# Q5 of the last two groups as seven 256x256x256 products, with its sums put together apart and added to the output in double tiles

## The reference

```python
W = L0_cond_weights[itok_B_0_15]                  # (64, 64, 64), one of 16 per batch element
y = einsum('bct,bcd->bdt', x, W)                  # conditioning, per batch element 64x64
xf = y.reshape(-1, 1024)                          # 4096 rows
scores = xf @ Wr.T                                # 64 experts of rank 16
top_vals, top_idx = top_k(scores, 16)
G = zeros((4096, 64)).at[rows, top_idx].set(softmax(top_vals))
h = einsum('nd,krd->nkr', xf, A)                  # 4096 x 1024 by 1024 x 1024
out = einsum('nkr,kdr->nd', h * G[:, :, None], B) # 4096 x 1024 by 1024 x 1024
return x + 2.0 * out
```

## Time and profile before

| | us |
|---|---|
| three runs | 708.48, 707.5, 706.84 (median 707.5) |
| the profiled execution | 707.46, of it span 705.7 |
| PE busy in the span | 700.4 (99%) |
| PEld busy | 608.5 (86%) |
| DVE busy | 568.8 (81%) |
| ACT busy | 292.2 (41%) |
| DMA | 301 GB/s on average |

### The profile page before, as it was taken

One profiled execution on the slowest core, in us unless ns is written; L12 is line 12 of the kernel. 1 busy time (PEld: TensorE's weight loads), 2 busy tenths in 40 slices (PEclk: granted clock), 3 DMA queues, 4 the chain that ended last, 5 costly groups with the idle time before them and its releaser, 6 DMA issues.

```text
span 705.7 us, 11098 instructions
## 1 busy us (share of the span) xinstructions
PE 700.4 (99%) x3822; PEld 608.5 (86%) x3822; DVE 568.8 (81%) x1022; ACT 292.2 (41%) x541; POOL 15.8 (2%) x22
## 2 busy tenths in 40 slices
PE   8999999999999999999999999999999999999998
PEld 8888888888888888988999888898899988888897
DVE  5888998897757899889795867987668496699885
ACT  5575554534535541444333542242334364233220
POOL 0000000100000000010000000001000000000100
PEclk9999999999999999999999999999999999999999
DMA  8976679787899998979989775868769987666886
GB/s 314 405 291 279 211 281 401 229 261 268 332 382 417 415 359 290 406 255 325 388 312 412 285 271 189 301 247 245 248 274 372 380 311 258 199 217 211 228 329 239
DMA packets 68937, 212.35 MB, mean 301 GB/s; under 512 B 10706, under 2 KB 13394, under 8 KB 68242
## 3 DMA queue, kind: packets, MB, share of 16 engines
q1 hardware_dynamic: 64802, 204.30, 78.0%
q0 software_dynamic: 2304, 4.20, 3.9%
q10 hardware_dynamic: 1776, 3.15, 1.2%
HBM read 150.80 MB, written 65.01 MB: 306 GB/s over the span
## 4 chain that ended last, share of the span: by engine, by line
PE 99%; DMA 1%; DVE 0%; issue 0%; DVEq 0%
PE Pb L755 40%; PE Pb L788 29%; PE Pb L809 13%; PE Cb L737 8%; PE S L852 4%; PE Pb L831 3%; DMA xc<-in_wts 1%; PE S L844 1%; PE T L907 0%; PE T L913 0%; PE Pb L771 0%; PE Cb L866 0%; PE S L866 0%; PE T L866 0%; DVE Q L1212 0%
## 5 line engine op out<-in xcount | busy, mean ns | idle before, releaser
L755 PE MATMUL Pb<-Op,Wt 128*128 128x512 f32 x888 | 214.2, 391 | 0.0
L755 PEld LDWEIGHTS Pb<-Op,Wt 128*128 128x128 f32 x888 | 165.4, 188 | 33.9
L788 PE MATMUL Pb<-Wt,Op 128*128 128x512 f32 x744 | 179.7, 391 | 0.0
L788 PEld LDWEIGHTS Pb<-Wt,Op 128*128 128x128 f32 x744 | 138.1, 188 | 28.1 <-DVE Op L1212 0.4
L1212 DVE TENSOR_TENSOR Q<-Pb,Q 128x512 f32<-128x512 f32 (+1 forms) x105 | 92.8, 901 | 27.9 <-issue 17.5
L1212 DVE TENSOR_TENSOR Op<-R,Op 128x512 fp32r<-128x512 f32 x100 | 66.6, 686 | 23.4 <-ACT Op L945 23.3
L755 PE MATMUL Pb<-Ox,Wt 128*128 128x512 f32 x300 | 75.3, 390 | 0.0
L998 ACT COPY R<-Cb 128x512 f32<-128x512 f32 x60 | 35.1, 587 | 91.2 <-PE Cb L737 91.2
L755 PEld LDWEIGHTS Pb<-Ox,Wt 128*128 128x128 f32 x300 | 56.0, 188 | 11.5
L945 ACT CAST Op<-R 128x512 fp32r<-128x512 f32 x100 | 58.3, 622 | 17.3 <-DVE R L1212 10.4
L1212 DVE TENSOR_TENSOR Cq<-Pb,Cq 128x1024 f32<-128x1024 f32 (+1 forms) x46 | 44.5, 966 | 24.3 <-issue 10.4
(11 more groups left out here) (118 smaller groups left out, 688.9 us busy)
## 6 DMA issues: line engine op xcount, KB each, us to landing
Wt<-Wd SPq DMA_DIRECT2D x201, 512.0 KB, 6.5
Wd<-Wt SPq DMA_DIRECT2D x56, 512.0 KB, 5.1
xc<-in_x SPq DMA_DIRECT2D x24, 512.0 KB, 5.4
Q<-in_x SPq DMA_DIRECT2D x16, 512.0 KB, 5.3
out<-Q SPq DMA_DIRECT2D x8, 1024.0 KB, 4.8
BR<-in_B SPq DMA_DIRECT2D x4, 1024.0 KB, 8.5
Q<-in_x SPq DMA_DIRECT2D x16, 256.0 KB, 5.6
out<-in_x SPq DMA_DIRECT2D x16, 256.0 KB, 5.9
```

The lines of the kernel that those rows point to most:

```text
L755: t = e.matmul(Pb[:, j, :], Wt[:, k, a, 128 * c:128 * c + 128], part((USES1[m], s, c), z), start=fresh and (c, a, z) == (0, 0, 0), stop=(c ...
L788: t = e.matmul(Pb[:, i, :], part((USES2[m], s, c), a)[:, 128 * i:128 * i + 128], Wt[:, k, z, :], start=fresh and (c, a, z) == (0, 0, 0), s ...
```

## The change

In groups 2 and 3 `TWO` becomes (0, 4, 5, 6): Q5, too, is computed in seven forms. For this:

- seven more made units (level 5) are made in the first half of group 2, in steps 12 to 15 (P3) and 20 to 22 (P7). Their source T1b, a weight sum that group 0 computes, is stored to a DRAM tensor in group 0 and read back into BR in group 2;
- S1 is split in seven pieces; its four sums (`sum_five`) are made in Q4's stage (in group 3 two of them in Q7's), on semaphore v_ysum;
- Q5's forms use the banks of `BANK1` (3, 0, 3, 2, 3, 2, 3). They aren't added to Q but put together in Cq[:, 0], S1's place: ScalarE copies forms 0, 2, 3 and 6, VectorE adds forms 1, 4 and 5 (`drain_five`);
- the whole is then added to Q by four adds of a double tile (128x1024, `add_five`), two into Q5's place and two into Q3's, which stand in Q3's stage at steps 0, 1, 2 and 4. At steps 0 and 1 they stand ahead of the splits, and Q3's drain stands behind these;
- the splits of S1, S4 and the next group's y21 are spread anew over Q4, Q5 and Q3 on VectorE (`lows_second`), and `sum_y` moves within Q5's stage;
- the two 1 MB stores of rows 0 to 3 move from Q5's stage to steps 0 and 3 of Q3's, behind `add_five`;
- the first form of the next group's P2 waits for ScalarE's copy of Q5's form 6.

```diff
-TWO = [(), (0, 4, 6), (0, 4, 6), (0, 4, 6)]
+TWO = [(), (0, 4, 6), (0, 4, 5, 6), (0, 4, 5, 6)]
-LEVEL = (4, 6, 0, 7)
+LEVEL = (4, 6, 0, 7, 5)
+           7: [8, 9, 10, 12, 13, 14, 20], 5: [12, 13, 14, 15, 20, 21, 22]}
 def splits_second(s, m, c):
-        return [("G22", c + 5)] if c < 2 else [("S1", c - 2)] if c < 6 else []
+        return [("G22", c + 5)] if c < 2 else [("S1", c - 2)] if c < 6 or 5 in TWO[s] else []
+    if m == 5 and m in TWO[s]:
+        return [("S1", c + 5) if c < 2 else ("S4", c - 2)]
+def lows_second(s, m, c):
+    if 5 not in TWO[s] or m < 4:
+        return splits_second(s, m, c)
+    if m == 4:
+        return [("G22", c + 5)] if c < 2 else [("S1", c - 4)] if c > 3 else []
+    if m == 5:
+        return [("S1", c + 3)] * (c < 4) + [("S4", k) for k in ((), (), (0,), (), (1,), (2,), (3, 4))[c]]
+    return [("S4", c + 5)] if c < 2 else [("y21", k) for k in ((), (0,), (), (1,), (2, 3, 4))[c - 2] if s + 1 < NS]
...
+                        if (s, step) == (2, 6):
+                            e.wait_ge(v_made, 28)
+                            e.wait_ge(l_b[1], 32)
+                            e.wait_ge(l_b[2], 32)
+                            e.dma_start(raws[2], T1b).then_inc(l_b[4], 16)
+                        if s == 0 and step in (17, 19):
+                            n = (step - 17) // 2
+                            e.wait_ge(v_bsum["T1b"], 2 * n + 2)
+                            e.dma_start(T1b[:, 2 * n:2 * n + 2, :], BR[:, 0, 2 * n:2 * n + 2, :]).then_inc(l_b[1 + n], 16)
+                        if 5 in TWO[s] and m == 6 and i in (0, 3):
+                            n = 1 if i == 0 else 0
+                            e.wait_ge(v_out, out_done(s, 5, n, 1))
+                            q_store(s, 2 * n, 0, 1024)
+                        if m == 5 and m in TWO[s]:
+                            continue
...
+                if m > 4 and 5 in TWO[s] and k in (0, 1, 3):
+                    if m == 5:
+                        e.wait_ge(v_out, out_done(s, *{0: (3, 3, 1), 1: (4, 1), 3: (4, 5)}[k]))
+                    else:
+                        e.wait_ge(v_out, out_done(s, *{0: (4, 6), 1: (5, 1), 3: (5, 5)}[k]))
...
+                        elif m == 5 and m in TWO[s] and i in (0, 2, 3, 6):
+                            e.wait_ge(p_two, form_done(s, 5, i))
+                            e.wait_ge(v_lo["S1"], split_done("S1", s, {0: 0, 2: 1, 3: 5, 6: 5}[i]))
+                            e.wait_ge(v_ysum, s1sum_done(s, "t4"))
+                            e.copy(five(i), Pb[:, BANK1[i], :].rearrange("p (i n) -> p i n", n=256)).then_inc(a_out, 1)
...
+            def drain_five(s, r):
+                if r in (1, 4, 5):
+                    e.wait_ge(p_two, form_done(s, 5, r))
+                    e.wait_ge(*in_output(s, 5, {1: 0, 4: 3, 5: 2}[r]))
+                    add(five(r), Pb[:, BANK1[r], :].rearrange("p (i n) -> p i n", n=256), five(r), v_out)
+            def add_five(s, n, name):
+                e.wait_ge(v_out, out_done(s, 5, 5))
+                e.wait_ge(*in_output(s, 5, 6))
+                tile, half = INTO[name][0] + 2 * n, INTO[name][1]
+                to = Q[:, tile:tile + 2, 512 * half:512 * half + 512]
...
+                add(to, Cq[:, 0, 2 * n:2 * n + 2, :], to, v_out)
...
+                            if m > 4 and 5 in TWO[s]:
+                                if m == 6 and c == 0:
+                                    add_five(s, 1, "Q5")
+                                elif m == 6 and c == 1:
+                                    add_five(s, 0, "Q3")
+                                if m == 6 and c > 1:
+                                    drain_two(s, m, c)
+                                for name, k in lows_second(s, m, c):
+                                    lo(name, s + (name == "y21"), k)
+                                if m == 6 and c < 2:
+                                    drain_two(s, m, c)
+                                elif m == 6 and c == 2:
+                                    add_five(s, 0, "Q5")
+                                elif m == 6 and c == 4:
+                                    add_five(s, 1, "Q3")
+                                if m == 5:
+                                    if c < 2:
+                                        sums_two(s, 6, SUMS2[c + 2])
+                                    drain_five(s, c)
+                                    if 1 < c < 6 and s + 1 in ONE:
+                                        sum_y(s + 1, SUMS2[c - 2])
```

More of the change, by code:

```diff
@@ L99, in ones, with fives @@
     return sum(r in ONE for r in range(s))
+def fives(s):
+    return sum(5 in TWO[r] for r in range(s))
 def cond_step(s, m, i):
@@ L232, in level_before, with sums_before, ysum_done, s1sum_done @@
     return sum(len(TWO[r]) for r in range(s)) + TWO[s].index(m)
+def sums_before(s, m):
+    return 4 * (level_before(s, m) - fives(s + (m > 5)))
 def y21_done(s, c):
     return 4 * s + 4 * ones(s) + c + 1
+def ysum_done(s, name):
+    return 4 * (ones(s) + fives(s)) + SUMS2.index(name) + 1
+def s1sum_done(s, name):
+    return 4 * (ones(s + 1) + fives(s)) + SUMS2.index(name) + 1
+def banks_two(m):
+    return BANK1 if m == 5 else BANK2
 def split_done(name, s, c):
@@ L257, in outs @@
                 copied += [(s, m, i, 0) for i in range(4)]
+            elif m == 5 and m in TWO[s]:
+                copied += [(s, m, i, 0) for i in (0, 2, 3, 6)]
+                order += [(s, m, i, 0) for i in (1, 4, 5)]
+            elif m == 6 and 5 in TWO[s]:
+                order += [(s, 5, 1, 1), (s, 6, 0, 0), (s, 5, 0, 2), (s, 6, 1, 0), (s, 6, 2, 0), (s, 5, 0, 1), (s, 6, 3, 0),
+                          (s, 6, 4, 0), (s, 5, 1, 2), (s, 6, 5, 0), (s, 6, 6, 0)]
             elif m in TWO[s]:
@@ L458, in out2, with five, places2 @@
             return Q[:, tile + 2 * n:tile + 2 * n + 2, at:at + 256]
-        def places2(m):
+        def five(r):
+            t, n = INTO2[r]
+            return Cq[:, 0, 2 * n:2 * n + 2, 256 * t:256 * t + 256]
+        def places2(m, s):
+            if m == 5:
+                return Cq[:, 0, :, :], Cq[:, 1, :, :] if s + 1 < NS else y(1, 0, 4)
             return ((Cq[:, 1, :, :], Cq[:, 3, :, :]) if m == 4 else (Cq[:, 2, :, :], u[:, :, :]) if m == 6 else
@@ L650, in _ @@
                                 made_store(k, MADE_AT[k].index(step - 1))
+                        if s == 2 and step - 1 in MADE_AT[5]:
+                            made_store(5, MADE_AT[5].index(step - 1))
+                        if (s, step) == (2, 6):
[3 more added lines that the diff above has]
+                            e.dma_start(raws[2], T1b).then_inc(l_b[4], 16)
                         if (s, step) == (1, 9):
@@ L956, in made_hi @@
                     e.wait_ge(*stored(m, n - 4))
+                elif m == 5:
+                    e.wait_ge(l_b[4], 48)
+                    if n < 2:
+                        e.wait_ge(p_cond, rows_number(2, 6 + n, 0))
+                    else:
+                        e.wait_ge(v_lo["S4"], split_done("S4", 1, 6))
                 elif m == 0:
@@ L1067, in hi_second @@
                 elif name == "G22":
-                    e.wait_ge(v_two, 4 * level_before(s, 4) + SUMS2.index(FORMS[c]) + 1)
+                    e.wait_ge(v_two, sums_before(s, 4) + SUMS2.index(FORMS[c]) + 1)
+                elif name == "S1" and (5 not in TWO[s] or FORMS[c][0] == "b"):
+                    e.wait_ge(v_s1, 4 * s + 4 if 5 in TWO[s] else 4 * s + c + 1)
                 elif name == "S1":
-                    e.wait_ge(v_s1, 4 * s + c + 1)
+                    e.wait_ge(v_ysum, s1sum_done(s, FORMS[c]))
                 elif name == "S4" and (6 not in TWO[s] or FORMS[c][0] == "b"):
@@ L1128, in _ @@
                                 made_hi(k, MADE_AT[k].index(step))
+                        if s == 2 and step in MADE_AT[5]:
+                            made_hi(5, MADE_AT[5].index(step))
                         if m == 0 and s in ONE:
@@ L1278, in sum_y, with sum_five @@
                     add(quarter(to, "t4"), quarter(b, "b21"), quarter(to, "t2"), v_ysum, ALU.subtract)
+            def sum_five(s, name):
+                (b, to), n = places2(5, s), s1sum_done(s, "t1")
+                if name == "t1":
+                    e.wait_ge(v_s1, 4 * s + 4)
+                    if s + 1 < NS:
+                        e.wait_ge(v_lo["G22"], split_done("G22", s, 5))
+                    else:
+                        e.wait_ge(v_lo["T4"], 4 * s + 4)
+                    add(quarter(to, "t1"), quarter(b, "b12"), quarter(b, "b11"), v_ysum, ALU.subtract)
+                elif name == "t2":
+                    e.wait_ge(v_ysum, n)
+                    add(quarter(to, "t2"), quarter(b, "b22"), quarter(to, "t1"), v_ysum, ALU.subtract)
+                elif name == "t3":
+                    add(quarter(to, "t3"), quarter(b, "b22"), quarter(b, "b12"), v_ysum, ALU.subtract)
+                else:
+                    e.wait_ge(v_ysum, n + 1)
```

(15 more changed lines are left out.)

50 lines of the change are left out of this document (33 added, 17 removed).

## The result

The changed kernel takes 709.13 us (median; 708.53 to 710.13), the kernel before, run in turn with it, 707.5 (706.84 to 708.69). The ratio is 1.0024, with a 95% interval of 1.0016 to 1.0033: 1.6 us slower. The forecast was 707.8, 0.3 us slower, so the time lies inside the range and 1.3 us above the point, just over the line of 0.2% that divides "the same" from "slower". The profiled execution took 710.09 us, of it span 708.3.

What follows compares the result with a forecast made beforehand. TensorE's matmuls were taken to bound the kernel, with VectorE's slack spent by the change: 707.46 - 1.66 (saving) + 1.3 + 0.6 (stalls in groups 2 and 3) + 0.1 (semaphores) = 707.8 us; range 705.8 to 709.2.

Steps and rivals of the forecast that it cites:

- the same: Outcome between 706.1 and 708.9 us, within 0.2% (1.4 us) of the kernel before; 55%.
- TensorE's saving: Q5's matmuls as seven forms: 0.89 us saved in group 2, 0.77 in group 3, 1.66 in all.
- DVE's order as the bound: VectorE, nearly full, drains Q3's forms late and TensorE waits: 1.3 us in group 2, 0.6 in group 3.
- on time at form 4: VectorE keeps up through Q4 and Q5 and still waits for Q5's form 4 when TensorE ends it.
- The semaphore's way: Handover from VectorE to a waiting TensorE: six stalls at 0 to 0.1 us, 0 to 0.6, taken 0.1.
- the walk: VectorE's operations in order from the end of Q5's form 4; Q3's form 0 drained 6.73 us later in group 2.
- The tail: Last stores at the kernel's end, done just ahead of the last one: 0 to 0.8 us, taken 0.
- Edits costed at nothing: Seven made units (0 to 0.5 us uncovered), T1b's store and reading back (0 to 0.5, taken 0), SP's stores, the tail.
- (a): Rival: the gain arrives whole, TensorE never waits, 705.8 us; 25%.
- (b): The stalls in Q3's stages as summed, 707.8 us, from 706.9 up to 708.6; 50%.
- (d): Rival: DVE falls behind already in Q4 or Q5, 2 x 0.6 us more, 709.0 us; 10%.
- (c): Rival: weights land late behind stores at the seam to group 3, TensorE stalls 1.8 us, 709.6 us; 15%.

Runs made afterwards that it cites:

- no_adds: The changed kernel without the four double-tile adds in Q3's stage, so Q5 is missing from its output; 706.51 us, ratio 0.9990 to the kernel before.
- split_behind: The changed kernel with VectorE draining Q3's forms 0 and 1 before each step's split, not after; 708.96 us, ratio 1.0021 to the kernel before.
- reorder: The changed kernel with VectorE's work in Q3's stage in a new order and stores at other steps; 707.53 us, ratio 0.9998 to the kernel before.
- pool_adds: A further reordered version of the changed kernel, with GpSimd doing the two adds into Q5's own place; 714.46 us, ratio 1.0091 to the kernel before.
- prep_only: The changed kernel with made units, their stores and T1b kept, but Q5 one product again; 707.17 us, ratio 0.9998 to the kernel before.

## Why the prediction was right, and where it was off

**TensorE's saving** was right: 1.66 forecast, 0.78 + 0.87 = 1.65 measured (1.61 by the chain). The new stage in group 2 is 13.63 against 13.52 worked out, so the 0.89 of this step was 0.11 too much; group 3's 0.77 was 0.10 too little.

**DVE's order as the bound** was right, in its place and its mechanism. DVE is on time at form 4, all of Q4 and Q5 pass without a wait of TensorE, the long stalls are before Q3's third form in both groups, and they are put down to DVE's adds into Q. That the work in the queue causes them and not one operation's place is shown by no_adds (no stalls) and split_behind (the stall splits into two).

**The semaphore's way was mis-sized**, the one term that moved the result. "Six stalls at 0 to 0.1 us, taken 0.1" was reasoned from the 0.20 us between TensorE's end and a drain. The other way measures 0.83 us from a drain's start to TensorE's restart, in six places: both groups of the change, twice in split_behind, once in reorder, once in pool_adds (0.82). That is 0.23 over the 0.60 of the walk, and DVE pays 0.22 itself where an add waits for the drain right before it: each once per group, 0.9 us in all. The other 0.2 of the 1.1 over the walk's 1.9 are the 0.06 or 0.07 behind each long wait and, in group 3, a double-tile add that starts 0.09 later behind ScalarE's copy than worked out. So the waits are 1.22 and then 0.63 us in group 2 (forecast 1.0 and 0.35), and 0.57 and then 0.64 in group 3 (0.25 and 0.35). Over the stages of before that is 1.77 and 1.27, together 3.04 where the sum has 1.3 + 0.6 + 0.1 = 2.0. The trace of before had a nearer row than the one that was taken, outside the three stages that were read: in Q5 of group 3 a sum into u on VectorE, and ScalarE's cast of u, which waits for it.

```profile
682.35 0.69 DVE L1212 TENSOR_TENSOR u<-Cq 128x512 f32<-128x512 f32 x1
...
683.13 0.62 ACT L945 CAST Op<-u 128x512 fp32r<-128x512 f32 x1 [7.23 <-DVE u L1212]
```

The waiting engine starts 0.78 us behind the start of the sum, 0.18 over the 0.60. By it four handovers would have been 0.7 instead of 0.1, and the forecast 708.4. The 0.83 of the way to TensorE itself stands in no row of before, since no row of TensorE waits for a drain there.

**The tail** was taken at 0 within 0 to 0.8, and is 0.3. With the measured losses put in, 707.46 - 1.66 + 3.04 + 0.3 = 709.1, the measured median.

**Edits costed at nothing** hold: prep_only shows that the made units, T1b's way through DRAM and ScalarE's new wait are covered.

**The rivals.** (a), the gain whole, falls by TensorE's rows. (b) holds in its mechanism, but the time is above the 708.6 given as its upper end, which had semaphores at 0.1 us each; the range held it only by the room left for (d), which didn't happen, and that is luck. By the forecast's own line (slower above 708.9) the time falls in the outcome that had 20%, not in the 55% of "the same". (c), late weights at the seam, isn't in the changed kernel. It was the right thing to watch, though: in no_adds, with Q3's stage 1.7 us shorter and the stores where the change has them, it appears. (d), DVE late in Q4 or Q5 already, falls by the 1.79 us that DVE waits at form 4.

## What to carry to other kernels

Where a change gives more work to an engine that has little slack, walk that engine's program order from its last wait to the next point where somebody waits for it, and price each handover: here 0.83 us from the start of a 0.6 us operation to the restart of the engine behind it, and 0.2 us where an operation waits for the one before it on its own engine. If the queue is too full for its stretch, moving one operation can only move the stall, as here; writing the order of the whole stretch anew, with what nobody waits for put last, took it away. A gain ahead of the very end is worth only what the last stores let through: look first which of them leave early because the engine that feeds them has nothing else to do.
